# A decoder on one Trainium2 core: another order of the same steps on every engine

## The reference, cut to what matters

```
x = LN(x + attention0(x))                 # causal, one head, on LN(x)
x = LN(x + long_convolution(x, ctx))      # 16 heads of 8 channels, outer products of x and ctx
x = LN(x + ternary_ffn(x))                # 256 -> 2 x 1024 -> 256, weights and rows quantised
x = LN(x + decayed_linear_attention(x))   # projections, running sum over the rows, group norm
x = LN(x + cross_attention(x, ctx))       # 16 heads of 128, 4 key/value heads, rms norm on q and k
x = LN(x + geglu_ffn(x))                  # float8, 256 -> 2 x 1024 -> 256
```

## Time and profile before

| what | us |
|---|---|
| median of 3 runs | 990.24 |
| lowest of them | 990.1 |
| the profiled execution | 989.49 |
| its span | 987.7 |
| TensorE busy in it | 870.5 |
| VectorE busy | 726.7 |
| ScalarE busy | 490.4 |
| GpSimd busy | 260.3 |

### The profile page before, as it was taken

How to read it: one execution, slowest core, us unless ns; L and a number is a source line. 1 busy time by engine, 2 the same in 40 slices (tenths; PEclk the granted TensorE clock), 3 DMA queues, 4 the chain that set the end, 5 groups by cost and what they waited for, 6 DMA issues and landing times.

```text
span 987.7 us, 14447 instructions
## 1 busy us (share of the span) xinstructions
PE 870.5 (88%) x5066; PEld 688.7 (70%) x5066; DVE 726.7 (74%) x1735; ACT 490.4 (50%) x1249; POOL 260.3 (26%) x298
## 2 busy tenths in 40 slices
PE   5756669998989899998999999999999999999964
PEld 4534557786778667976788677876688768777742
DVE  2769857968696879787868777977877876754543
ACT  3354123555543575347542665328642575476742
POOL 0417113223152220513134211531134211310100
PEclk9868788999999999999999999999999999999985
DMA  7752100010001000010001000010000000000000
GB/s 258 247 185 96 22 11 1 12 22 1 22 1 23 0 12 22 1 22 1 22 12 22 1 12 11 11 22 1 23 1 1 1 12 1 1 2 11 11 11 11
DMA packets 37064, 28.67 MB, mean 29 GB/s; under 512 B 18688, under 2 KB 34560, under 8 KB 36608
## 3 DMA queue, kind: packets, MB, share of 16 engines
q1 hardware_dynamic: 36992, 27.74, 9.1%
HBM read 25.64 MB, written 2.10 MB: 28 GB/s over the span
## 4 chain that ended last, share of the span: by engine, by line
PE 40%; DVE 35%; ACT 11%; issue 9%; POOL 2%; DMA 1%; SPq 1%; DVEq 0%; POOLq 0%; ACTq 0%
PE bank L941 6%; PE bank L1121 5%; PE bank L1211 4%; DVE S L870 4%; ACT S L567 3%; PE bank L1128 3%; PE bank L1200 3%; PE bank L1190 2%; DVE S L877 2%; PE bank L1114 2%; PE bank L1000 2%; DVE mx L873 2%; PE bank L1001 2%; DVE amax L759 2%; DVE X L633 2%
## 5 line engine op out<-in xcount | busy, mean ns | idle before, releaser
L567 ACT ACTIVATE S<-S,mx 128x128 f32<-128x128 f32 x256 | 99.4, 392 | 59.7 <-DVE mx L873 59.4
L1121 PE MATMUL bank<-XTE,w_xq 128*128 128x256 f32 x512 | 124.1, 386 | 2.9 <-ACT QA L541 1.9
L1211 PE MATMUL bank<-w_xo,OX 128*128 128x256 f32 x512 | 116.0, 380 | 0.0
L540 ACT ACTIVATE QS<-bank,per_partition_sb 128x256 f32<-128x256 f32 x128 | 60.4, 472 | 99.3 <-PE bank L1121 97.9
L1121 PEld LDWEIGHTS bank<-XTE,w_xq 128*128 128x128 f32 x512 | 94.6, 192 | 20.3 <-ACT QA L541 5.0
L1211 PEld LDWEIGHTS bank<-w_xo,OX 128*128 128x128 f32 x512 | 95.7, 190 | 14.7 <-issue 1.9
L870 DVE SCALAR_TENSOR_TENSOR S<-bank,rq,xmask 128x128 f32<-128x128 f32 x256 | 71.7, 342 | 17.5 <-PE bank L1190 14.9
L332 POOL TENSOR_TENSOR rq<-vq,minus_half 128x8 f32<-128x8 f32 x32 | 52.4, 1639 | 119.6 <-DVE vq L843 119.6
L231 POOL TENSOR_TENSOR prod<-XTA,ccolA 128x256 f32<-128x256 f32 x96 | 63.9, 695 | 47.0 <-PE bank L1001 34.4
L1190 PEld LDWEIGHTS bank<-KTX,QA 128*128 128x128 f32 x512 | 64.6, 194 | 13.2 <-issue 10.8
L1190 PE MATMUL bank<-KTX,QA 128*128 128x128 f32 x512 | 68.4, 279 | 2.2 <-ACT OX L576 2.2
(11 more groups left out here) (219 smaller groups left out, 1864.4 us busy)
## 6 DMA issues: line engine op xcount, KB each, us to landing
xin<-in_x SPq DMA_DIRECT2D x8, 256.0 KB, 2.7
cnat<-in_ctx SPq DMA_DIRECT2D x8, 256.0 KB, 2.7
ccolA<-in_ctxT SPq DMA_DIRECT2D x32, 64.0 KB, 2.7
taps_sb<-in_taps SPq DMA_DIRECT2D x1, 2048.0 KB, 10.9
ccolE<-in_ctxT SPq DMA_DIRECT2D x16, 128.0 KB, 2.3
w_xq<-in_L_xattn_Wq SPq DMA_DIRECT2D x1, 2048.0 KB, 11.3
w_xo<-in_L_xattn_Wo SPq DMA_DIRECT2D x1, 2048.0 KB, 16.2
out_x<-X SPq DMA_DIRECT2D x8, 256.0 KB, 2.1
```

The lines of the kernel that those rows point to most:

```text
L567: ins = nc.scalar.activation(S[:, b, seq(h)], S[:, b, seq(h)], ACT.Exp, bias=mx[:, b, h:h + 1], accum_out=sm[:, b, h:h + 1])
L1121: ins = nc.tensor.matmul(cols(EQ)[:, h], w_xq[:, k, hh * XDIM:(hh + 1) * XDIM], XTE[:, k], start=k == 0, stop=k == HALVES - 1)
L1211: ins = nc.tensor.matmul(rows(EY)[:, b], OX[:, h, b], w_xo[:, n * XGROUP + h], start=n == 0 and h == 0 and b == 0, stop=n == XKV - 1 and h ...
```

## The change

All five strings of `ORDER` are written anew. Each has the same number of each letter as before (711 letters for PE, 687 for DVE, 501 for ACT, 187 for POOL, 39 for SP), so each engine has the same steps, and those of one station keep their sequence; the stations interleave otherwise.

```diff
--- before.py
+++ after.py
@@ -1223,38 +1223,38 @@
 
 ORDER = {
     "pe": (
-        "sassaasaaaasaaaaaaaasasaacaqcqaacacaacaaaacaaccacacccacacacacaqqcqcaaqcaqacqxaqyacqxaqyxaqycaqyxaccq"
-        "coqcyxaqccqcyqcxycqxqcqyaoqxyqxycqcxaqcxyqxycqaocqayqaxqoqcaaqyaaqyaxaccycxqaxacaqccacqaycxocqaycqax"
-        "yaqxoqaycqyacxqyaxaxacaqoqcxyqxycaqxaqayqcxoqayxqaccqcaqayaaycqcacaxcaqacqacaqcayqyxoaxyqaxqacyqoacx"
-        "aqxycxaqaacaxqycqxoqyaxyqaqcaqccyqcaxoaqcyxcqyaayqacaxcaqacaqcaaqcayqayxqxaqaocqxaycaqxaoyxycxyqaaoc"
-        "qaxcayqxyqxoqyqxqaxyqacaqccaqcayqycxcacacaaqcaqcaacaqayaqyxqxaqoaqxayoxqcayxcyaxcyqacoqxaqacxyaqyaqy"
-        "qxqoqcayxqyaaccqcayxaqxocaqccacaqcacaaqacayqyaxaxyqxaqoqxyqxyqxyqcocxyqxycqxocqyqcqxayqxyaqcyqccxqco"
-        "qcyqccqcyqcxycxqxacqyayoqxyqxaqxoqaaxqayxyqxaqyoqxaqyxaqyaqyxqaoqyxaqyxqyxaaqaaoxqyxyxyaoaxyayxaoaaa"
-        "aaaaaaaaaaa"
+        "sassaasaaaasaaaaaasaaasqcqacaaccaaccaaccacaaacacccacacacaqqqcaqcqacqxaycqqcxyqyaxqaocyqccqcxaqacqccy"
+        "qcyaqcyacaqaycqyaqaqxaaxxaqoqyxqxaxcqaacyqoacayqcyxaxacqxaaaqyaqacyqaccacoaycqcacxcqaxycqacxaqycaqxa"
+        "oqxcyaaxqaaqycoyxqcyaxqaxcyqycxaqxoqacoqaxyqccqacqaaxqayacyayqcaqaacaqcyaxqycxocqyacaqxayqayqxcqacxq"
+        "oqaacxqaaxcqyxcqoqxaqxaqyacyxqyccqacoayqycxqaycaaxaqcxacaqacaqcaayqcyaxqxqaoaqyxacqoacyxayxqcaxaqaya"
+        "qoxcqyxycaqxayqaoqycxqyaxqcacycqxoacaqcyaayaqcaycaaqcaqacxqxyacyxqoqyaxaxqacqxayqycaqocaqxaqaqaxyqcx"
+        "qocqyaqyayqaccqccaxqaxyqcyacaacaacxaqacaqacaqcqaxoqyxaxocqacqxyacqyxcqxycqaoqxyqyxyqcxqccoqcxayqycqc"
+        "yxqcxcayqaaoqcyxcaqyxqcqxyaoqyxqayqxaqxyaqyqaxqoqyxaaqxoyqyaxqxayqxqaoqyaxqyqyxaqxayqyaoxayxaaxaoyxy"
+        "xoaaaaaaaaa"
     ),
     "dve": (
-        "aasasasassaaasaassaaaaaaaaaaaaaasasassaascassacaqaqcaqacacaaacacaacaacaacaaaacaaacacaaacacccacaccacc"
-        "cacaqacqaaaqaxacyxaayacacacacaacqaaxyaxccycaqaacacccycqcxqycqxaccqcyyxcxqcqqcaaccyaxyacxoaqacaoaacaa"
-        "aaacycyacxaaaxaqaccaacacacccqaccyqxyacqxaqaaaycxaaxyacaqacqaqxccxcyacyaocoacaqcaaaacaayycaacaaxacqxa"
-        "acaacacaacaqcaccyqaxyqaxqacaaaxcaxacaqayqacycqaxcxccacayccyoaqoacaayaaycaaxacqxaacaaacacaaacaacqaaqc"
-        "qcqaxayxacyaaaxycxycqacqaqxacaxyaoyaocccaqaccacyaxycxacacaaaaqcaaccaaaacaacaaaaqqaqacqxayxcyacaxcyxa"
-        "aaqcqycaqcayxayacaxoacqcoacacyayxacxaqccacaacacaaaacaaacaacqaaaayqxyqaxqaccxyqxycqqcxoxcyoyccccqcyac"
-        "xycxcqcccqcyccqxyacqxacqyaxaaxqyqaqxayxaoyoaaqxyaxyaqaayxaaxyaqxyxyaaaoaoaaaaaaaaaaaaaa"
+        "aasasasassaaaasasasaaaaaaaaasaasasasasasasccaqaqaqcacacaccccacaacaacacaaaaaaacccacaacacaacacaccaaaqq"
+        "cqcxycxayacccccaqacycxcaaxqycccaacyacaayacqaacqacaqaaqaaaaxaxaacacaqyqxyaxcaqcaacyaaycacaacaacaacaax"
+        "aacaacaxcaqoayocaycaccqacxcaxcaccacqaayxqayaxqacaqacayyxcxcacqacqccqaxaycxacaacayoaaaaoaaqyacayaaaac"
+        "aacaqacxcxcycaycacqcqaqaqxaacxcaacqayxaqxaqcaccycacxaycxcycoaqoayacyaaaaacxacaaqxaacaaacacaaacaqcacq"
+        "caqyxaqxyacaaaxayaxcaqyacaqaqccxycyaxcacooaccaqcyaaxycxaaaaaacaacaaaaqcaayacaycacxaqccxcqayqayqxaaxc"
+        "aaqqcqaayacaxayocaccccqaxoayccyacaqacaaacaaacxaaaaxaacaacacaaqcqacaccqxyqxaycaccqxyqxcyqccccxycaxoyc"
+        "aocqaacyyxccqxaccacyaqycqxcxqqyaayxaqxqaqaayxyoxoaaqayxyxaqyayxaqxaaayaxayxaooaaaaaaaaa"
     ),
     "act": (
-        "sssaaasasassssscaacascascacsccccccccaaaacqqcqcacccxqycqxcqxyqyccxqyqcxyccqyqxyxycqxyqxcycqaxacxyccax"
-        "ycqacqyqxqacyqyxcxyqxcccqyxqayaxcayxaycqyaaxcxaaqyxcqccxyxycaxacqqcxyaqaxyqcaqycyqccxqqyxcyaxyaxacqy"
-        "acxaaxqcaxaccqxycycxyyqxaaqcqacqaxycyxcqyaqycxqqyxcaaxcyqaxcayqxaayxycxaacqycxcycxyxqqxyqxyqaacacaqy"
-        "qcycxacqqyxcxayqaxyxqcayxcyacxcqaacyxaacxycyqqyqxqcxyyaacaqaxyqxcaccqqyyxxyxqxycqxyqxcycxyxyccxcqqyc"
-        "qxcyaqxyacqcyqxcyqccqyxxyaxyayqxqxaaqxyaxayxyxqyqxaqyxaqyaqxayqxyaaxyqaayxqxyxyaxyaxyayxaaaaaaaaaaaa"
+        "sssaaasasassssscscscaascaccacccaccccqcqqccaacccxqyqacxyqcaxyqccqyaqxcccyqyqyyqxxxqcyqxxcyaxacayacycc"
+        "xaqxycqcqyqccxycqcycxqxayaaxqaqxcaayxcaayxycyxqccxqyaacyxqcxcaxyacqcxqayqxqycycyqcqyxxyqayaqacxyaxca"
+        "aqcxqaacxqcxcycyxxcqxaaycqayqcxyaqyycxqacyxqcxqyqxcaxyaacqxyacyxaaxqaayqcxycxcyxyccaaxqyaqycxqayxqca"
+        "cyqcxyyqcqyxqxyxcyaxaxyaqcayqxacaqyacaxcxqcyqxcqycqyaacacqayxqxycaccxqqxycxaxcqycaqxyacqcxcycxyacxyy"
+        "qxqcqcxyqxayacyqcxyqcaxayqyxqxyyaxyxqaqxyaqyaxaxayqxyqaaxyqyxqxqyaxqyxayqxayqayxaayxaxayxyxyxaaaaaaa"
         "a"
     ),
     "pool": (
-        "sasaaaaaaaacsqaqaacacaacaacccacaaqcaaacqcaqaccqcqcqqccaaaqoaaacqcaccqcqqacaqcoaaqacacaaqccaqcqqcaqac"
-        "coaqacaaqaaccqacqqcqcaaoqcaacaaqcaacqaqcqcqcaaoqcaaaqcacaacqqaqcqcocqcqcqccqqqaoqqaqoaa"
+        "sasaaaaaaacsaqqcacaacaaacccacaqccaqacaqcacaaqcqqacaqcaaacaaacqocaqcccqaqaqccqaaacaoaaqcaqcccqqqcaqac"
+        "coaqaacaaaqccaqcqqaqcacoacaqacaaaqcacqcqqqcaaocqcaaqacaaacqcacqqcqcocqcqcaqcqqqoaqqqaoa"
     ),
     "sp": (
-        "asasqsasassasaaqaqaaoqaaoqaaoqaaqoqoooo"
+        "assaqsassassaaqaaaqaoaqaoqaaoqaaoqqoooo"
     ),
 }
```

## The result

The kernel after takes 945.54 us (median of 4 executions, 942.16 to 949.84). The kernel before took 990.1, 990.24 and 993.04 us beside it; the ratio is 0.9537 with a 95% interval of 0.9515 to 0.9558. 980.0 was forecast, with a range of 965 to 992. The profiled execution took 947.48 us with a span of 945.7. Two executions that stand far outside all others, 2268.74 us of before and 1803.29 us of e4_middle, are in no ratio here.

The account below looks back on a forecast made before the run. TensorE, 95% busy, was taken as the bound from 203 to 949 us, with VectorE busiest from 50 to 145.5. Start 8.4, middle 0 and tail 1.4 gave 9.8 us off the median 990.2: 980 us, range 965 to 992.

Parts of the forecast that it names:

- The middle of the kernel: Between 203 and 949 us: the new order wins zero, with bounds from 20 us less to 13 us more.
- The start: Up to c1.dxT: it comes 20 us earlier with 11.6 us more TensorE work behind it, 8.4 us won.
- the first stretch: From 50 us to q0.xT: q0.xT comes 12 us earlier, 7 from moved VectorE steps and 5 from idle time.
- The second: From q0.xT to c1.dxT: some 15 us of VectorE steps go behind; none of its 8.7 us idle taken off.
- The wait of 5 us or more at c0.q3T0: Sign expected in the changed profile: TensorE waits 5 us or more at this step of middle 0.
- The tail: After o7.y3: 4.2 us won, less 1.5 for lost cover and 1.3 for a table load, net 1.4 us.
- 5.4 us of ffn 6: In the tail: this work, before after o7.y3, moves ahead of it; 35.5 us against 39.7, 4.2 won.
- the cover that x7 and y7 lose: In the tail: x7 and y7 end with nothing left to cover them, costing some 1.5 us.
- rival (3): TensorE's clock falls from 50 to 145.5 us, gain gone or 1000 us; chance 0.08, shared with a worst-bound middle.
- Rival (1): More is won: VectorE's idle time fills and the middle gains a few us, 966 us; chance 0.24.
- idle time between c1.dxT and o7.y3 moves by over 10 us: Falsifier: the prediction is wrong if this idle time moves that much either way; an idle share near 5% was expected.
- The two rules: Tail's table load is followed at once by the Gelu, 1.30 us, without a drain; waits make TensorE's next burst start cold.

Follow-up runs that it names:

- e4_middle: Kernel before, with the sequence of the kernel after only from q1.xT to q7.xT, start and tail as before: 964.24 us, ratio 0.9725.
- e10: Kernel before with the output projection (TensorE) on 128 of 256 columns from group 2 on: 993.33 us, ratio 1.0016.
- e5: Kernel before with 66 ready TensorE steps moved ahead of waiting ones between 203 and 944 us, other engines unchanged: 1004.22 us, ratio 1.0125.
- e2: Kernel before up to 232.5 us (q1.xT), then the sequence of the kernel after: 957.29 us, ratio 0.9656.
- e1: Kernel after up to 217 us (q1.xT), then the remaining steps in the sequence of the kernel before: 993.47 us, ratio 1.0017.
- e17: Kernel after with steps shifted by small distances on all engines, so steps ready sooner by median durations stand earlier: 964.08 us, ratio 0.9724.
- e18: Kernel before with steps shifted by small distances on four engines, so steps ready sooner by median durations stand earlier: 971.15 us, ratio 0.9797.
- e12: Kernel before with the fronts' z and r steps (VectorE) on half of their columns from group 2 on: 989.25 us, ratio 0.9977.
- e6: Kernel before with scaling and quantising of the ternary ffn (VectorE) on half of the columns from group 2 on: 986.40 us, ratio 0.9946.
- e19: Kernel before with the scores' exponentials (ScalarE) done for two of four heads from group 2 on: 984.23 us, ratio 0.9934.

## Why the prediction was wrong

**The step that failed** is "The middle of the kernel": "both orders leave nearly nothing uncovered for groups 2 to 5, so I take zero", bounded by 20 us less. It measured 31 us less (46.6 lost before, 15.5 after). It rested on the sentence ahead of it, "TensorE works 95% of the time and is the bound". e10 shows that it was not: 40 us less of its work gave nothing, though its busy time fell by 22.6 us. What was done about cover was to look one round trip at a time; a step's wait depends on all queues that its round trip passes, and e5, where steps ready by the trace were moved ahead and the time grew, shows that even the wait on one queue can't be mended from that queue. The lower bound was built from the best 100 us of the order before, as if another order couldn't do better than this one at its best; after's window from 500 to 600 us has 0.5 us idle, against 2.1.

What took the place of it: a wait before the change was mostly a step at the head of a queue that waited while another station's step behind it was ready (by the semaphores' times in the traces, 28.5 of the 36.2 us idle from c1.dxT to o7.y3; 5.6 of 14.8 after). That the order of the queues in the middle decides, and neither the start nor the work of one engine, is shown by e2 and e4 (27 to 34 us from whole sequences) beside e1 and the single cuts. That it takes all four queues together is what e5 (TensorE's queue alone: 12.8 us slower) and e17 and e18 (small shifts on four queues: 18.5 us slower and 20.8 faster) speak for; no run changed VectorE's or ScalarE's queue alone, so this is not shown. Not settled is how much of the middle's 31 us is the layout: fit alone won 7.5 there, and the layout with a spoilt fit still stood 14 better than before (32.3 against 46.6). The new layout also has the middles back to back (on VectorE, between c.no1 of one and c.ug of the next, 35 us from the end of middle 2 on before and 3 after; ahead of middle 2 it has a break of 15 us that the old one hasn't). But e17 keeps that, 4 us, and loses 17 us more, and cheaper fronts (e12) gave 2; so as a cause it is only argued.

**The start**: 12 us earlier at q0.xT was forecast, 14.3 measured (145.50 to 131.24); VectorE's idle time from 50 us to q0.xT fell from 24.0 to 18.0, 6 us for the 5 taken. c1.dxT came 17.3 us earlier (20 forecast) with 11.0 us more work behind it (11.6). Net 6.3 against 8.4. The mechanism held in the first stretch, which brought 2.3 us more than forecast. The second brought 3.0 us for the 8 forecast (20 less 12), so it was over-sized by 5 us: VectorE's busy time in it fell by 8.4 us (48.83 to 40.47), but its idle time rose from 8.7 to 14.1 us, where the prediction had allowed for 0 to 4 us less. The wait of 5 us or more at c0.q3T0 came (7.04), and q0.k0 waits 3.52 us for the last big weight, of which the prediction had warned. Yet e1 says that this term is not money in hand: handed to before's sequence it was gone by q1.xT.

**The tail**: from the end of o7.y3 31.4 us follow (945.7 - 914.27), and 30.1 + 1.3 was forecast; f7.xT waits 3.81 us, the Gelu's table load is there and on the last chain (931.20 to 932.49). The term gave 4.1 in place of 1.4, because the "5.4 us of ffn 6" that moved ahead are elapsed time: as TensorE work they are 3.5 us. And the cover that x7 and y7 lose cost 0.6 us for the 1.5 taken (lost time grew by 2.3 us from x7.sc0 to o7.y3 before, by 2.9 after).

**The rivals**: the clock of rival (3) didn't decide: 0.75 from 50 us to q0.xT (0.78 before). A lower clock behind more waits shows in another place, e10. Rival (1) was nearest with 966 us, but gave the middle "a few us", and was still 20 us too slow. The falsifier "idle time between c1.dxT and o7.y3 moves by over 10 us" is what happened: by 21.4.

**The two rules.** The table load of the tail ends as the Gelu starts, 1.29 us from one start to the other. The Trainium skill, "ScalarE: Activation LUTs", section "What ACT_TABLE_LOAD costs", counts a drain besides; this trace shows none, as the earlier trace rows did. As to the clock, c0.dxT without a wait ahead now takes 0.60 us at a granted clock of 1.00 (before it took 1.09 us at 0.50, behind a wait of 3.83 us), and q0.xT behind 4.45 us still takes 1.08 at 0.50. The Trainium skill, "TensorE: Matmul & The Clock Gate", section "HAM oscillation", has waits make the next burst start cold; these rows agree.

## What to carry to other kernels

Where every engine runs a fixed list, don't price a reordering by the busy share of the fullest engine: 95% busy with 36 us of waits may be 36 us to win. Before trusting "it is the bound", take some of that engine's work out and look at the time: 40 us less gave nothing here. A low share of the chain that ended last (40% here) is a hint and no price. Taking work out of such an order may give little; a change of one queue alone cost 12.8 us and changes of four gave 20 to 45, so try them together, and treat a gain at one place as real only at the end of the kernel. Where bounds come from windows, remember that they describe the order that made them.

## What the runs showed of the hardware

Less TensorE work went with a lower TensorE clock: with 40.1 us taken out the mean granted clock of the profiled execution went from 0.949 to 0.933 and the remaining matmuls took 17.5 us longer. The executions without that cut agree: 19 of before on the same chip had 0.944 to 0.949, ten of e10 had 0.928 to 0.938. Cuts on VectorE or ScalarE alone didn't do it (e6 0.941 to 0.946, e19 0.944). Three cuts together had 0.929, and in the window from 203 to 903 us both have 0.97 where the kernel before has 0.99 (before, then e10, columns of the earlier trace rows):

```profile
203.00:903.00 700.00, 664.72 (x3944) 531.78 (x3945) 540.92 (x1314) 371.27 (x992) 195.76 (x210) 0.99 0.04 10
```

```profile
203.00:903.00 700.00, 642.91 (x3907) 513.85 (x3908) 539.58 (x1310) 369.54 (x991) 193.94 (x209) 0.97 0.04 10
```

The opposite shows too: the kernel after, with fewer waits, has 1.00 from q1.xT to x7.sc0.
